# Attention step: three of four key tiles as two fp16 parts, all low parts on VectorE, every second step's edge mask on GpSimd

## The reference, cut to what matters

```python
def _L0_gnn_ref(features, adj, Wq, Wk):           # features = layernorm(x)
    Qn = _cos_normalize(features @ Wq.T)
    Kn = _cos_normalize(features @ Wk.T)
    raw_att = Kn @ Qn.T
    att = jnp.where(adj > 0, raw_att, NEG) * TEMP
    att = jax.nn.softmax(att, axis=1)
    prop_fea = att @ features
    ...
def _L1_gnn_ref(input, adj, M, W, b, a):
    ...
    mask = (adj[:M] > 0) & valid[None, :]
    ...
    return att @ inp
```

## Time and profile before

| what | value |
|---|---|
| median of 3 runs | 797.28 us |
| profiled execution, its own time | 796.37 us |
| span of its instructions | 794.6 us |
| TensorE busy over the span | 728.0 us (92%) |
| VectorE, ScalarE, GpSimd busy | 550.5, 514.0, 181.7 us |
| first and last masking instruction of the attention start at | 67.4 and 429.6 us |

### The profile page before, as it was taken

One profiled execution on the slowest core, in us unless ns is written; L12 is line 12 of the kernel. 1 busy time (PEld: TensorE's weight loads), 2 busy tenths in 40 slices (PEclk: granted clock), 3 DMA queues, 4 the chain that ended last, 5 costly groups with the idle time before them and its releaser, 6 DMA issues. The chain is left out here.

```text
span 794.6 us, 11783 instructions
## 1 busy us (share of the span) xinstructions
PE 728.0 (92%) x3621; PEld 431.9 (54%) x3621; DVE 550.5 (69%) x1590; ACT 514.0 (65%) x791; POOL 181.7 (23%) x222
## 2 busy tenths in 40 slices
PE   1947999999999999999998599999999999989997
PEld 1743444444444444444443489775555566678875
DVE  7785667877787787878787647866567554656526
ACT  1846888888888888888886477853223444424345
POOL 2450000000000000000000064300354465576760
PEclk9989999999999999999999799999999999999999
DMA  5208999999987887979782400005011221225108
GB/s 139 79 1 236 303 292 251 288 250 302 262 263 225 259 245 221 254 236 268 226 252 80 144 4 1 1 1 133 19 38 42 79 65 49 65 76 140 35 24 288
DMA packets 97950, 121.93 MB, mean 153 GB/s; under 512 B 8518, under 2 KB 76371, under 8 KB 97632
## 3 DMA queue, kind: packets, MB, share of 16 engines
q1 hardware_dynamic: 93856, 113.72, 50.0%
q0 software_dynamic: 4032, 7.47, 2.9%
HBM read 87.48 MB, written 34.60 MB: 154 GB/s over the span
## 5 line engine op out<-in xcount | busy, mean ns | idle before, releaser
L578 DVE SCALAR_TENSOR_TENSOR probs<-adj,probs 128x1024 f32<-128x1024 int32 x128 | 156.7, 1224 | 82.0 <-ACT probs L551 78.3
L501 PE MATMUL ps<-x,qT 128*128 128x512 f16 x768 | 187.9, 382 | 3.2 <-PEq L228 3.2
L551 ACT ACTIVATE probs<-ps 128x1024 f32<-128x1024 f32 x128 | 130.9, 1023 | 50.9 <-PE ps L501 50.9
L562 ACT ACTIVATE mask<-probs 128x1024 fp8e4<-128x1024 f32 x128 | 134.0, 1047 | 0.0
L513 PE MATMUL ps<-probs,v 128*128 128x512 f32 x256 | 130.7, 592 | 0.0
L501 PEld LDWEIGHTS ps<-x,qT 128*128 128x128 f16 x768 | 75.4, 98 | 94.7 <-issue 5.5
L1528 PE MATMUL ps<-mask,parts 128*128 128x512 fp8e4 x512 | 116.9, 379 | 0.0
L584 DVE TENSOR_TENSOR p_lo<-probs,p_hi 128x512 f16<-128x512 f32 x128 | 87.5, 684 | 0.1
L798 POOL MEMSET hT<- 128x128 f32 x1 | 0.2, 204 | 378.0 <-POOLq L454 378.0
L559 ACT ACTIVATE p_hi<-probs 128x512 f16<-128x512 f32 x128 | 79.6, 622 | 1.7 <-DVE probs L578 1.7
L1887 POOL DMA_INDIRECT mixed_spill<-mask x70 | 70.2, 1003 | 38.1 <-issue 28.8
(11 more groups left out here) (323 smaller groups left out, 1031.1 us busy)
## 6 DMA issues: line engine op xcount, KB each, us to landing
adj<-in_adj SPq DMA_DIRECT2D x128, 512.0 KB, 4.5
sorted_rows_spill<-blank SPq DMA_DIRECT2D x32, 528.0 KB, 7.0
sorted_rows_spill<-blank SPq DMA_DIRECT2D x14, 330.0 KB, 8.2
mask<-sorted_rows_spill SPq DMA_DIRECT2D x35, 132.0 KB, 2.3
mask<-mixed_spill SPq DMA_DIRECT2D x7, 512.0 KB, 7.0
mask<-in_x SPq DMA_DIRECT2D x4, 512.0 KB, 6.3
feat_spill<-mask SPq DMA_DIRECT2D x8, 256.0 KB, 2.0
x_feat<-in_x SPq DMA_DIRECT2D x8, 256.0 KB, 4.4
```

Source lines behind the costliest of these rows:

```text
L501: ins = nc.tensor.matmul(out, qT[:, q_half, j], kT[:, c, k_half * GROUP:(k_half + 1) * GROUP], start=(n == 0), stop=(n == 2))
L551: nc.scalar.activation(probs[:, k % RING, :], ps[:, b:b + 2, :].rearrange("p b n -> p (b n)"), ACT.Exp, scale=1.0 / QK_SCALE ** 2).then_in ...
L562: nc.scalar.activation(mask[:, k * W:(k + 1) * W], probs[:, k % RING, :], ACT.Sign, saturate=False).then_inc(mask_kept, 1)
L578: nc.vector.scalar_tensor_tensor(out=probs[:, k % RING, :], in0=adj[:, k % LOADS, :], scalar=0.0, in1=probs[:, k % RING, :], op0=ALU.is_gt ...
```

## The change

- Of four key tiles (two steps) now one is multiplied in fp32 and three as two fp16 parts. Even steps are as before. In odd steps both tiles have fp16 parts, and the fp32 matmul is gone. `v32` holds a quarter of the tiles, `v16` three quarters.
- ScalarE's high part and VectorE's low part are 128x1024 in odd steps, 128x512 in even ones.
- ScalarE's `keep_mask` is left only in even steps. In odd steps GpSimd writes the mask straight from adj: `(adj > 0) * 56.0` as a byte, and the byte 56 read as fp8 is 1.0.
- Adjacency has three places in place of four. A place used by an odd step must also have been read by GpSimd before it is loaded again.

```diff
                 def keep_values(g, u):
-                    two = bass.ds(g * 2, 2)
-                    nc.gpsimd.tensor_copy(v16[:, two, 0, 0:D - 1], pairs(feat[:, u, :, :])[:, :, 1, 0:D - 1]).then_inc(v_hi_ready, 1)
-                    nc.gpsimd.tensor_copy(v32[:, two, 0:D - 1], pairs(feat[:, u, :, :])[:, :, 0, 0:D - 1])
+                    one, three = bass.ds(g, 1), bass.ds(g * 3, 3)
+                    nc.gpsimd.tensor_copy(v16[:, three, 0, 0:D - 1], feat[:, u, 1:SUB, 0:D - 1]).then_inc(v_hi_ready, 1)
+                    nc.gpsimd.tensor_copy(v32[:, one, 0:D - 1], feat[:, u, 0:1, 0:D - 1])
...
-        LOADS = 4
+        LOADS = 3
...
                     if k >= LOADS:
                         sp.wait_ge(masked, k - LOADS + 1)
+                        if (k - LOADS) % 2:
+                            sp.wait_ge(mask_by_pool, (k - LOADS + 1) // 2)
...
+                for k in range(1, STEPS, 2):
+                    pool.wait_ge(adj_landed[k % LOADS], 16 * (k // LOADS + 1))
+                    nc.gpsimd.tensor_scalar(sb["mask"][:, k * W:(k + 1) * W], adj[:, k % LOADS, :], 0.0, ONE_F8, ALU.is_gt, ALU.mult).then_inc(mask_by_pool, 1)
+                pool.wait_ge(mask_by_pool, STEPS // 2)
...
                 def gather(k):
...
-                    nc.tensor.matmul(out, v32[:, jp, :], probs[:, k % RING, 0:GROUP], start=(jp == 0), stop=False)
-                    pe.wait_ge(hi_ready, k + 1)
-                    nc.tensor.matmul(out, v16[:, jp, 1, :], p_hi[:, u, :], start=False, stop=False)
-                    nc.tensor.matmul(out, v16[:, jp, 0, :], p_hi[:, u, :], start=False, stop=False)
-                    pe.wait_ge(lo_ready, k + 1)
-                    nc.tensor.matmul(out, v16[:, jp, 0, :], p_lo[:, u, :], start=False, stop=(jp == PAIRS - 1))\
-                        .then_inc(pair_used, 1)
+                    if jp % 2 == 0:
+                        v = 3 * (jp // 2)
+                        nc.tensor.matmul(out, v32[:, jp // 2, :], probs[:, k % RING, 0:GROUP], start=(jp == 0), stop=False)
+                        pe.wait_ge(hi_ready, k + 1)
+                        nc.tensor.matmul(out, v16[:, v, 1, :], p_hi[:, 0, :], start=False, stop=False)
+                        nc.tensor.matmul(out, v16[:, v, 0, :], p_hi[:, 0, :], start=False, stop=False)
+                        pe.wait_ge(lo_ready, k + 1)
+                        nc.tensor.matmul(out, v16[:, v, 0, :], p_lo[:, 0, :], start=False, stop=False).then_inc(pair_used, 1)
+                    else:
+                        v = 3 * (jp // 2) + 1
+                        pe.wait_ge(hi_ready, k + 1)
+                        for h in range(2):
+                            nc.tensor.matmul(out, v16[:, v + h, 1, :], p_hi[:, 1 + h, :], start=False, stop=False)
+                            nc.tensor.matmul(out, v16[:, v + h, 0, :], p_hi[:, 1 + h, :], start=False, stop=False)
+                        pe.wait_ge(lo_ready, k + 1)
+                        nc.tensor.matmul(out, v16[:, v + 1, 0, :], p_lo[:, 2, :], start=False, stop=False)
+                        nc.tensor.matmul(out, v16[:, v, 0, :], p_lo[:, 1, :], start=False, stop=(jp == PAIRS - 1)).then_inc(pair_used, 1)
...
-                    nc.scalar.activation(p_hi[:, k % SLOTS, :], probs[:, k % RING, GROUP:], ACT.Copy).then_inc(hi_ready, 1)
+                    if k % 2 == 0:
+                        nc.scalar.activation(p_hi[:, 0, :], probs[:, k % RING, GROUP:], ACT.Copy).then_inc(hi_ready, 1)
+                    else:
+                        nc.scalar.activation(p_hi[:, 1:3, :].rearrange("p h n -> p (h n)"), probs[:, k % RING, :], ACT.Copy).then_inc(hi_ready, 1)
...
                     keep_high(k)
-                    keep_mask(k)
-                act.wait_ge(mask_kept, STEPS)
+                    if k % 2 == 0:
+                        keep_mask(k)
+
+                act.wait_ge(mask_kept, STEPS // 2)
...
                 def keep_low(k):
                     dve.wait_ge(hi_ready, k + 1)
-                    nc.vector.tensor_tensor(p_lo[:, k % SLOTS, :], probs[:, k % RING, GROUP:], p_hi[:, k % SLOTS, :], ALU.subtract)\
-                        .then_inc(lo_ready, 1)
+                    if k % 2 == 0:
+                        nc.vector.tensor_tensor(p_lo[:, 0, :], probs[:, k % RING, GROUP:], p_hi[:, 0, :], ALU.subtract).then_inc(lo_ready, 1)
+                    else:
+                        nc.vector.tensor_tensor(p_lo[:, 1:3, :].rearrange("p h n -> p (h n)"), probs[:, k % RING, :],
+                                                p_hi[:, 1:3, :].rearrange("p h n -> p (h n)"), ALU.subtract).then_inc(lo_ready, 1)
```

More of the change, by code:

```diff
@@ L265, in keep_values @@
                     pool.wait_ge(feat_ready, g + 1)
-                    two = bass.ds(g * 2, 2)
-                    nc.gpsimd.tensor_copy(v16[:, two, 0, 0:D - 1], pairs(feat[:, u, :, :])[:, :, 1, 0:D - 1]).then_inc(v_hi_ready, 1)
-                    nc.gpsimd.tensor_copy(v32[:, two, 0:D - 1], pairs(feat[:, u, :, :])[:, :, 0, 0:D - 1])
+                    one, three = bass.ds(g, 1), bass.ds(g * 3, 3)
+                    nc.gpsimd.tensor_copy(v16[:, three, 0, 0:D - 1], feat[:, u, 1:SUB, 0:D - 1]).then_inc(v_hi_ready, 1)
+                    nc.gpsimd.tensor_copy(v32[:, one, 0:D - 1], feat[:, u, 0:1, 0:D - 1])
                     pool.wait_ge(v_hi_ready, g + 1)
-                    nc.gpsimd.tensor_tensor(v16[:, two, 1, 0:D - 1], pairs(feat[:, u, :, :])[:, :, 1, 0:D - 1],
-                                            v16[:, two, 0, 0:D - 1], ALU.subtract).then_inc(v_lo_ready, 1)
+                    nc.gpsimd.tensor_tensor(v16[:, three, 1, 0:D - 1], feat[:, u, 1:SUB, 0:D - 1], v16[:, three, 0, 0:D - 1],
+                                            ALU.subtract).then_inc(v_lo_ready, 1)
                 pipelined(pool, GROUPS, [(0, keep_values)], slots=RING)
@@ L419, in attend @@
         STEPS = GROUPS * PAIRS
+        ONE_F8 = 56.0
         BLANKS = E * N // (STEPS // 4)
@@ L426, in attend @@
         probs = buf("probs", [P, RING, W])
-        p_hi = buf("p_hi", [P, SLOTS, GROUP], F16)
-        p_lo = buf("p_lo", [P, SLOTS, GROUP], F16)
+        p_hi = buf("p_hi", [P, 3, GROUP], F16)
+        p_lo = buf("p_lo", [P, 3, GROUP], F16)
         sumsT = buf("sumsT", [P, GROUP])
@@ L446, in attend @@
         pair_used = sem("pair_used")
+        mask_by_pool = sem("mask_by_pool")
         sums_copied = sem("sums_copied")
@@ L506, in gather @@
                     c, jp = divmod(k, PAIRS)
-                    u = k % SLOTS
                     out = ps[:, SUM_BANK + c % 2, :]
@@ L2205, in build @@
             with ExitStack() as attention:
-                sb["v32"] = attention.enter_context(nc.sbuf_tensor("v32", [P, PAIRS, D], F32))
-                sb["v16"] = attention.enter_context(nc.sbuf_tensor("v16", [P, PAIRS, 2, D], F16))
+                sb["v32"] = attention.enter_context(nc.sbuf_tensor("v32", [P, GROUPS, D], F32))
+                sb["v16"] = attention.enter_context(nc.sbuf_tensor("v16", [P, 3 * GROUPS, 2, D], F16))
                 sb["turn"] = attention.enter_context(nc.sbuf_tensor("turn", [P, D + 1], F32))
```

## The result

The changed kernel takes 871.66 us (median of 5 runs) against 798.49 for the kernel before (5 runs): 1.093 times as long, 95% interval 1.0894 to 1.0967, +73 us. The profiled execution took 876.97 us, the slowest of the five, with a span of 875.0. From its first to its last masking instruction the attention takes 438.0 us in place of 362.2; what follows takes 368.9 in place of 365.0. So nearly all of it lies in the attention. A pair of steps takes 6.90 us in place of 5.70.

A forecast was written before the change was run, and what follows sets the result against it. TensorE was taken to set the time, 5.70 us a pair; VectorE's load and loop with GpSimd's hold gave +14 to +45, middle +29.5, plus 0.7 in `prepare`: +30 on 797, 827 us, range 808 to 880.

The forecast's parts named there:

- the port: Attention, VectorE beside GpSimd: VectorE held while GpSimd works, 0.98 us per pair added, +14 to +45 us, middle +29.5.
- GpSimd's length: GpSimd's new odd-step mask instruction: taken as 1.17 us at a copy's pace, ends 0.90 and 2.49.
- The sum: Attention per pair: VectorE's load 5.92 us or its loop 6.40 against 5.70; with small parts, +30 us in all.
- the new wait on SP: SP's adjacency loads waiting for GpSimd's read: costs nothing while GpSimd finishes before VectorE, as in most steps.
- The rival of the three places: Adjacency loads: one in four late in the stage's first third, +14 us, 841 us; chance 0.07.
- The signs: What the later profile would show if the forecast were right or wrong, such as VectorE's stretched durations or load waits.
- GpSimd's length less 0.19: Rule for VectorE's hold: each GpSimd instruction adds its own time less 0.19 us, here 1.17 - 0.19 = 0.98.
- The slower-GpSimd rival: GpSimd's mask instruction slower than a copy: 855 us if it takes 1.6 us, 911 at 2.49; chance 0.28.
- TensorE's 12.8 us less: Odd steps' matmuls: one fp32 replaced by three fp16 saves 0.20 us each, 12.8 us over 64 odd steps.
- that loop: Attention: scores, exponentials, mask, VectorE's low part, its matmuls, next scores; 5.42 us for an odd step's low part.
- That alone would still fit: VectorE's wider low part in odd steps: 0.54 us more, 4.94 us per pair, said to fit without GpSimd.
- its relief: ScalarE in odd steps: lighter by more than half a microsecond through 64 fewer masks, counted as no gain.

The follow-up runs named there:

- e5: e1 with eight forms of GpSimd instruction (compare, product, copy, types, two inputs) run beside it in turn on the queries into scratch: 822.46 us in one execution.
- e3: The changed kernel with four adjacency places in place of three, one tile in four using another tile's values: 819.3 us, ratio 1.0307, stage 387.1.
- e7: The kernel before with three adjacency places in place of four and nothing else: 800.02 us, ratio 1.0028, stage 363.1.
- e4: e1 plus GpSimd's 64 compare-and-product instructions on the queries into an unread scratch tile, nobody waiting for GpSimd: 816.94 us, ratio 1.0279, stage 381.3.
- e11: e9 with VectorE's low part of odd steps at 512 columns again, the second tile using the first's low part: 783.64 us, ratio 0.9848, stage 350.2.
- e1: The changed kernel without GpSimd's masks: ScalarE writes every mask, SP doesn't wait for GpSimd, three places stay: 796.3 us, ratio 1.0018, stage 362.1.
- e9: e1 with four adjacency places and all values right, room taken from the sums' buffer: 796.08 us, ratio 0.998, stage 359.4.
- e12: e9 with ScalarE's mask left out in odd steps but the last, nobody making it: 795.45 us, ratio 0.9989, stage 359.7.
- e2: The changed kernel with GpSimd reading the queries instead of adjacency, starting after the previous step's mask, without SP's wait: 815.46 us, ratio 1.0264, stage 382.8.
- e8: The changed kernel with a plain GpSimd copy int32 to byte in place of compare and product: 831.0 us, ratio 1.0418, stage 399.3.

## Why the prediction was right or wrong

The sign was right, and so was the stage in which the time is lost, but the change was +73 us where +30 was forecast. That 871.66 lies inside the range is luck: its upper end, 880, was worked out for a GpSimd instruction of 2.0 us held at the port, and neither is what happened. The steps:

- **GpSimd's length: the step that failed first.** The sum took 1.17 us "because the instruction reads one tensor as the copy does", with 2.49 as the upper end. It takes 3.62. A copy was a good guide for a copy (1.04 in e5), and a TENSOR_SCALAR of one column showed its fixed part, but no row showed its slope. The upper end was too low as well. The estimate by the Trainium skill, "GPSIMD Engine Reference", section 3.1, 1.54 us, meets neither the copy nor this form.
- **What the length costs: the step that failed most.** "So the new wait on SP costs nothing while that holds." It didn't hold: SP waited for GpSimd 60 times, 208 us. The place costs 51 us of stage (changed kernel less e3; 52 by the medians), 39 of them by the length and 12 even with a short instruction. The rival of the three places named the resource, but had it at 14 us and without GpSimd's hold; e7 shows that alone it is at most 1 to 2.5 us. The signs were better than the sum: "If the time rises but VectorE waits for loads for most of it, the cause is the ring of three" is what happened, 45.6 of 76 us. "If GpSimd's instruction is over 2 us, only the size is wrong" is not.
- **The port.** The form was right (VectorE is held) and the size was 19 to 21 us in e4 where the sum had 14 to 45, middle 29. But the amount isn't GpSimd's length less 0.19. A hold lasts up to 0.88 us, beside an instruction of 3.62 us as beside one of 1.04, and only four of the 64 in the changed kernel held VectorE twice. The slower-GpSimd rival priced the length at the port: 855 at 1.6 us, 911 at 2.49. The time lies between them for a wrong reason; by this price 3.62 us would have given 827 + 2.45 x 64 = 984.
- **TensorE's 12.8 us less.** It is real (e11), and it is gone in e1 (stage 362.1 against 362.2), most of it to VectorE's wider low part (9.2 us, e9 less e11), the rest with the third place. The prediction saw that loop at 5.42 us, "already level with TensorE's 5.50", yet said of the low part "That alone would still fit". A pair takes 5.70 us in e1 and 5.66 in e9. TensorE's weight load waits for it in 57 of 64 odd steps of e1.
- **ScalarE.** Nothing for its relief: right here (e12, e2).

So the account of the stage closes: 0 us for fp16 parts with the wider low part (e1), 19 for the port (e4), 6 that e3 has over it, 51 for the place, in sum 76. By the medians it is 73; the profiled execution was the slowest of five. One thing is open in it. In this profile the granted clock was 0.96 in the stage, where TensorE had gaps (so a small part of it ran at the lower level), and 0.95 behind it, against 1.00 and 0.98 before; it was 1.00 in the stages of e3 and e8 too. So what the clock cost lies within the 51 us and the 39. TensorE is busy for 373.3 us in this stage and for 359.5 in e3's, with the same matmuls, so I estimate it at some 14 us or less. The clock wasn't tried by itself, nor were the 3.9 us behind the attention.

## What to carry to other kernels

Before an operation is moved to GpSimd, measure its very form: three forms that read one wide tile differ here by 3.5 times. When a second, slower reader is put on a ring of buffers (here the adjacency places), price the ring by the slower reader's length and by the queue that refills it in order, not by the port alone. And first check that the engine to be relieved bounds anything: leave the work out and look, as e12 does.

## What was not expected of the hardware

- A GpSimd TENSOR_SCALAR of 128x1024 takes 3.62 us with two operations, about 2.76 with one; a copy or cast 1.04 (e5, e8). Input as int32 or fp32 and output as byte or fp16 make no difference.
- VectorE with two SBUF inputs is held by GpSimd for at most 0.88 us, close to a copy's 0.88 ns for each of 1024 columns, though GpSimd works for 3.62. Beside a GpSimd instruction with two inputs it was held for 1.70 (e5). In the earlier trace rows, with two inputs read, hold and instruction had nearly the same length, and the two could not be told apart. That the hold is the read of the tile is my reading of the 0.88 and the 1.70 us; it was tried with one width alone.
- A small TENSOR_SCALAR of VectorE, with one SBUF input, was held in the first part of a GpSimd mask (line 637, 1.00 us at 377.19; GpSimd from 376.30 to 380.76, of which some 0.8 us were its own wait), ran as alone in the middle of another (line 637, 0.16 us at 479.19; GpSimd from 476.68 to 480.77), and was held again at the end of a third (line 90, 1.01 us at 172.63; GpSimd to 173.62). What the second hold is wasn't tried.

```profile
377.19 1.00 DVE L637 TENSOR_SCALAR denominator<-denominator 128x4 f32<-128x4 f32 x1
...
476.68 4.09 POOL L494 TENSOR_SCALAR mask<-adj 128x1024 uint8<-128x1024 int32 x1 [4.23 <-DMA adj<-in_adj]
...
479.19 0.16 DVE L637 TENSOR_SCALAR denominator<-denominator 128x4 f32<-128x4 f32 x1
```

- The Trainium skill, "SBUF — State Buffer", section "Who interferes with whom", says of VectorE in a 2-port mode and GpSimd that whoever issues first gets the shared pair for the whole instruction. These runs show no hold for the whole of GpSimd's instruction: within one of 3.62 us VectorE's low part takes its plain 0.68 us, and line 637 its plain 0.16. In which mode VectorE's instructions ran, no trace here says.
